# Idle TensorE products in layer 3's first pooling: five ahead of the wait for the pooled features in place of eight behind it

## What is computed

```python
for i in range(DEPTH):                          # DEPTH = 3
    xs.append(x)
    h = relu(_sage_layer(x, x, src, dst, emask, dWl1[i], dWr1[i], db1[i]))
    x = _sage_layer(h, h, src, dst, emask, dWl2[i], dWr2[i], db2[i])
    score = tanh(x @ w_ / norm(w_))
    vals, perm = jax.lax.top_k(score, k)        # k = ceil(n / 2): 625, 313, 157, 79
    x = x[perm] * vals[:, None]
    new_id = full((n,), -1).at[perm].set(arange(k))
    s2, d2 = (new_id[src], new_id[dst])
    emask = emask * (s2 >= 0) * (d2 >= 0)
    src, dst = (maximum(s2, 0), maximum(d2, 0))
    n = k
```

## Time and profile before

| | |
|---|---|
| median of 3 runs | 1033.14 us |
| the runs | 1032.57, 1038.27, 1033.14 us |
| profiled execution | 1034.62 us |
| its span, first to last instruction | 1032.8 us |
| mean granted TensorE clock | 0.962 |
| TensorE busy | 942.6 us (91%) |
| VectorE, ScalarE, POOL busy | 460.1, 281.9, 133.5 us |

### The profile page before, as it was taken

One profiled execution on the slowest core, in us unless ns is written; L12 is line 12 of the kernel. 1 busy time (PEld: TensorE's weight loads), 2 busy tenths in 40 slices (PEclk: granted clock), 3 DMA queues, 4 the chain that ended last, 5 costly groups with the idle time before them and its releaser, 6 DMA issues.

```text
span 1032.8 us, 15228 instructions
## 1 busy us (share of the span) xinstructions
PE 942.6 (91%) x5611; PEld 769.0 (74%) x5611; DVE 460.1 (45%) x1411; ACT 281.9 (27%) x631; POOL 133.5 (13%) x141
## 2 busy tenths in 40 slices
PE   7999998899999898799968988999999998899896
PEld 7996657799999666798847777777786554566785
DVE  6688565322223302522479996423343143222222
ACT  5111362122221114132437762332120111124010
POOL 2100000232221100144200000000102000000341
PEclk9999999999999899999989999999998999899998
DMA  9102001388984302277420000354001000232762
GB/s 330 80 1 61 1 1 51 126 331 302 333 321 133 128 5 119 76 263 265 127 99 23 1 1 1 123 183 152 1 1 32 1 0 5 119 122 70 259 218 71
DMA packets 27452, 117.08 MB, mean 113 GB/s; under 512 B 5478, under 2 KB 9484, under 8 KB 20223
## 3 DMA queue, kind: packets, MB, share of 16 engines
q1 hardware_dynamic: 21292, 98.65, 27.0%
q0 software_dynamic: 6096, 17.56, 5.1%
HBM read 102.83 MB, written 13.37 MB: 113 GB/s over the span
## 4 chain that ended last, share of the span: by engine, by line
PE 69%; DVE 16%; DMA 6%; issue 4%; ACT 3%; POOL 1%; SPq 1%; DVEq 0%; POOLq 0%; ACTq 0%
PE PS L756 7%; PE PS L435 6%; PE PS L581 5%; PE PS L814 4%; PE PS L771 4%; PE PS L1165 4%; PE PS L446 3%; PE PS L800 3%; PE PS L412 3%; PE PS L506 3%; DVE arena L1859 2%; PE PS L836 2%; PE PS L873 2%; DVE ring L1834 2%; PE PS L884 2%
## 5 line engine op out<-in xcount | busy, mean ns | idle before, releaser
L412 PE MATMUL PS<-const 128*128 128x128 f32 x824 | 107.2, 291 | 9.8 <-DVE X L1233 2.1
L412 PEld LDWEIGHTS PS<-const 128*128 128x128 f32 x824 | 102.7, 205 | 14.6 <-issue 4.2
L756 PEld LDWEIGHTS PS<-HT,ring 128*128 128x128 f32 x680 | 78.4, 192 | 3.4 <-issue 2.6
L756 PE MATMUL PS<-HT,ring 128*128 128x128 f32 x680 | 78.8, 275 | 2.2 <-DVE HT L1754 1.3
L2494 POOL DMA_INDIRECT slot_rows<-ST,route x46 | 46.5, 1011 | 168.5 <-ACT ST L2236 93.9
L2440 POOL TENSOR_TENSOR col<-col,power 125x5 f32<-125x5 f32 x8 | 9.5, 1182 | 435.7 <-DVE col L1248 347.9
L1751 DVE TENSOR_TENSOR HT<-HT,PS 128x256 f32<-128x256 f32 (+1 forms) x51 | 19.2, 377 | 93.6 <-ACT HT L2225 73.6
L958 PE MATMUL PS<-arena,HT 125*33 125x125 f32 x400 | 52.5, 279 | 0.0
L581 PE MATMUL PS<-HT 125*125 125x250 bf16 x470 | 51.3, 270 | 0.8 <-DVE HT L1616 0.8
L581 PEld LDWEIGHTS PS<-HT 125*125 125x125 bf16 x470 | 50.2, 136 | 0.9 <-DVE HT L1616 0.9
L771 PE MATMUL PS<-ring,HT 128*128 128x256 f32 x204 | 46.7, 379 | 0.0
(11 more groups left out here) (441 smaller groups left out, 1704.9 us busy)
## 6 DMA issues: line engine op xcount, KB each, us to landing
ring<-in_experts SPq DMA_DIRECT2D x17, 1386.0 KB
ring<-in_experts SPq DMA_DIRECT2D x17, 768.0 KB, 6.1
ring<-in_experts SPq DMA_DIRECT2D x11, 1026.0 KB
arena<-in_experts SPq DMA_DIRECT2D x6, 1026.0 KB
ring<-in_experts SPq DMA_DIRECT2D x6, 1024.0 KB, 8.9
arena<-in_experts SPq DMA_DIRECT2D x6, 1024.0 KB
arena<-in_gnn SPq DMA_DIRECT2D x5, 1024.0 KB, 5.9
ring<-in_experts SPq DMA_DIRECT2D x8, 513.0 KB, 3.7
```

Source lines behind the costliest of these rows:

```text
L412: pe.matmul(PS[:, bank, 0:128], ident, ident, start=True, stop=True)
L756: mm = pe.matmul(PS[:, bank, at:at + SLOTS], both[:, j, k, m * 128:(m + 1) * 128], xs[0][i % 2][:, k, :], start=(k == 0), stop=(k == KD - 1))
```

## The change

At level 0 the idle products at the end of the pooling are new: `stay_busy` with five, ahead of the wait of L1074 (L1075 in the changed kernel). At level 1 the eight at the head of the transposes are gone. For level 1 the new call has zero products, and no other call is touched.

```diff
-                    transposes(xin, rows_, busy=(14, 8, 0)[i])
+                    transposes(xin, rows_, busy=(14, 0, 0)[i])
...
                     if i < 2:
+                        stay_busy((7 if bank == 6 else 6) if i == 0 else 0, (5, 0)[i])
                         pe.wait_ge(xn_ready, n["xn"] + len(ks))
```

## The result

| | before | changed |
|---|---|---|
| median of 20 runs each | 1036.79 us | 1032.66 us |
| spread | 1032.57 to 1042.87 | 1027.60 to 1037.76 |
| profiled execution, span | 1034.62, 1032.8 us | 1030.42, 1028.6 us |
| mean granted clock | 0.962 | 0.963 |

The ratio is 0.9960, with a 95% interval from 0.9945 to 0.9975: of 1036.8 us that is 2.6 to 5.7 us saved. The forecast was 3.24 us. The three runs of before that the prediction had were at the low end of the twenty, so its absolute 1029.9 lies 2.8 us under what was measured, while the measured saving of 4.1 us lies 0.9 over its own.

What follows compares the result with a forecast made beforehand. TensorE's queue and clock were taken to bound the kernel. Eight products out (3.78 us) less 0.54 us for five put in saves 3.24 us: 1033.14 - 3.24 = 1029.9 us, range 1026.8 to 1032.9.

Steps and rivals of the forecast that it cites:

- the case it called likeliest: Around the first pooling: clock falls as recorded and returns 3.58 us after L435's start; 3.24 us saved, chance 0.60.
- a change that does nothing: Rival: added downstream dips or a late copy eat the saving; under 1 us remains, 1032.5 us, chance 0.06.
- the stretch: From L1061's end to L998's start, claimed to shrink from 14.8 to about 11.6 us; measured ones start at L1061's first product.
- Eight products out of the chain: L412, between wait and transposes: transposes could begin at 788.40 instead of 792.18, 3.78 us earlier.
- Five products into the gap: Behind L1061, ahead of the wait: ten records end at 788.94, delaying the transposes by 0.54 us.
- Transposes, copy, L435: After the wait: durations kept at 1.25, 0.51 and 7.68 us; L435 begins at 790.70 and ends at 798.38.
- VectorE's copies beside the products: Three copies beside the five idle products: no cost; as a bound, they end 0.18 us later.
- The gather hidden: Ahead of L998: POOL's gathered rows arrive about 795.7, before L435 ends at 798.38, with 2.7 us of cover.
- The cap on the gain: At L998: the gather's arrival at about 795.7 limits any gain to 5.9 us.
- The first rival: From L1061 to L998 the clock never falls; L998 waits for the gather, 5.9 us saved, 1027.2 us, chance 0.16.
- The second rival: In L435 the clock returns no earlier than 797.52; 2.2 us saved, 1030.9 us, chance 0.15.
- Downstream: Behind 801.62 everything moves up by the same amount; ±1.5 us allowed for clock dips that fall elsewhere.

Runs made afterwards that it cites:

- none: Kernel before with the eight idle products behind the wait taken out and none put ahead of it; 0.9948 of before, median 1033.50 us.
- five_third: The changed kernel unaltered, traced and timed a third time beside later kernels; 0.9954 of before, median 1034.81 us.
- wide64: Changed kernel with each index product of L1061 streaming its column 64 times over; 0.9968 of before, median 1031.50 us.
- wide128: Changed kernel with each index product of L1061 streaming its column 128 times over; 0.9976 of before, median 1031.84 us.
- inside12: Changed kernel plus twelve idle products among L1061's index products; first 1029.95 us in one run, then timed with a second trace at 0.9956 of before.
- copies_first: Kernel before without idle products in either place, VectorE's three pooled-tile copies moved ahead of the index's casts; 0.9971 of before, median 1033.11 us.
- five_and_eight: Kernel before with five idle products added ahead of the wait and the eight kept behind it; 0.9966 of before, median 1033.24 us.
- inside6: Changed kernel plus six idle products among L1061's index products, two ahead of each column; 0.9969 of before, median 1034.77 us.

## Why the prediction was right

The range held the time (1032.66 in 1026.8 to 1032.9, near its upper end), and the case it called likeliest is the one that happened in two of the changed kernel's three traces. That the absolute time fell inside, by 0.24 us, is luck in part. The base of the sum, three runs, lay 3.65 us under the later median of 1036.79; from that median the same saving gives 1033.55, outside the range. And the upper end stood there for a clock that comes back late or a change that does nothing, neither of which happened. What was right is the saving: 3.24 us forecast, 3.45 in the stretch, 4.1 timed.

- *Eight products out of the chain*: 3.78 us predicted for it. `none`, which does this alone, has a stretch shorter by 3.49 us; its transposes took 1.51 us instead of 1.25.
- *Five products into the gap*: predicted to end between 788.37 and 789.22 on before's clock, 0.54 us late. Ten records took 1.82 us and ended 0.26 us late. The price of a record was too high: from start to start it is 0.111 us at full clock in this trace and 0.215 at half, where the prediction had 0.152 and 0.237 from whole groups, ends included. So six records, not three, had started when the clock fell.
- *Transposes, copy, L435*: kept at 1.25, 0.51 and 7.68 us; 1.30, 0.51 and 7.76. The half-clock part of L435 was 796.21 - 792.36 = 3.85 us, predicted 3.58. This held in two of three traces of the changed kernel; in `five_third` the clock was back before L435 began, L435 took 5.93 us and the stretch lost 4.92 us, a case that the prediction doesn't list.
- *VectorE's copies beside the products*: costed at nothing, rightly; they took 1.08 us as before.
- *The gather hidden*: L998 waited only for L435. The cap on the gain was real: in `wide64`, `wide128` and the first `inside12` L998 did wait for the gather. But 5.9 us was too high. It took the fastest of the three landings, 4.2 us, for the last gather, and a DMA share of 0.00 for its end; in `wide64` the last gather was issued at 793.60 and landed 5.00 us later, and the cap measured 17.77 - 12.73 = 5.04 us.
- *The stretch*: "from 14.8 to about 11.6", counted from L1061's end; it went from 14.82 to 11.38.
- *The first rival*, the clock that never falls, was wrong for the changed kernel in all three traces. Its mechanism was right in `wide64`, where the clock held and the stretch lost 5.04 us against before; the 5.9 forecast for it shared the error of the cap. The rule of the Trainium skill named there ("TensorE: Matmul & The Clock Gate", section "Why this matters for your kernels", on idle gaps) isn't enough for this place: the clock fell with no gap at all.
- *The second rival*, that three products fewer delay the return: not in the traces of the changed kernel. `copies_first` showed something of it, where the work moved by 1.6 us and the clock followed by only 0.2.
- *Downstream*: I allowed 1.5 us for moved dips. That was too little for one execution: between this pair of traces they made -2.9 us behind the second pooling and +1.95 ahead of L1061, and single runs of either kernel spread over 10 us. The point inherited it through its base of three runs.

What stays open is why the measured 4.1 us is more than 3.45, if it is: the interval, 2.6 to 5.7 us, holds both.

## What to carry to other kernels

Read idle filler by its place: products between a satisfied wait and real work are paid in full and give back only what the clock returns, and the first thing to try is to have none. To keep TensorE's clock, go by what products stream, not by how busy the engine is recorded to be: a run of one-column products let it fall, and 64 columns for each cost 0.1 us in all and held it in the one trace taken. A clock kept in one place may fall in the next one; time the whole before believing the stretch.

## What the runs showed of the hardware that I had not expected

- The granted clock fell behind 2.94 us of back-to-back one-column f32 products, with TensorE recorded as busy throughout, in all nine traces where these were left plain; it fell 3.13 to 3.58 us after the first of them, a narrow band for nine executions. With 64 or 128 columns it did not fall there in either trace.
- What a one-column record costs goes by its stationary columns. From start to start at full clock, an f32 record of L1061 with 125 stationary columns (20 of the 30) took 0.109 us with 1 moving column, 0.109 with 64 and 0.111 with 128; with 63 stationary columns (the other 10) it took 0.057, 0.058 and 0.111. TensorE's weight loads were recorded as busy for 3.10 of 3.13 us there (`five_third`), so the weight load sets the pace until the moving columns outnumber the stationary ones: that is my reading of these six figures. The 0.098 and 0.152 us in the expectation of `wide64` are means over groups, of mixed forms and with their ends, which is why 4.4 to 4.7 us for `wide128` was too much.
- The next dip seems to move rather than go. In all traces in which L435 ran wholly at full clock but two (`five_and_eight` and the first trace of `inside12`), the clock fell again behind the transposes of L998, and L1008 took 9.78 to 11.39 us instead of 8.34. But it did so in `copies_first` and `inside6` too, where L435 had run partly at half clock. What decides it, the runs don't show.
